# Embedding, projections and out-projection around a first attention as streams of four tiles, with constant rows kept on chip

## The reference

```python
h = _L0_tok_ref(x, emb, Wq, bq, Wk, bk, Wv, bv, Wo, bo)
#   e = emb[x]; q, k, v = e @ W.T + b, 16 heads of 16
#   softmax(0.25 * q @ k.T) @ v, then @ Wo.T + bo
h = h + _L0_attn_ref(_layernorm(h), Wq, ..., Wqs, bqs, Wks, bks, Wvs, bvs, temp)
#   the same with a score of 16 + 3 products for each head:
#   three more come from small projections of q, k and v
#   (k-part and v-part crossed)
```

## Time and profile before

| | us |
|---|---|
| median of 3 runs | 4443.97 (4440.75 to 4445.12) |
| the profiled execution | 4443.18, span 4441.2 |
| start to the first score matmul | 128.0 |
| first attention | 408.4 |
| between the attentions | 198.6 |
| second attention | 408.6 |
| the rest | 3297.6 |

### The profile page before, as it was taken

One profiled execution on the slowest core, in us unless ns is written; L12 is line 12 of the kernel. 1 busy time (PEld: TensorE's weight loads), 2 busy tenths in 40 slices (PEclk: granted clock), 3 DMA queues, 4 the chain that ended last, 5 costly groups with the idle time before them and its releaser, 6 DMA issues. The chain is left out here.

```text
span 4441.2 us, 98171 instructions
## 1 busy us (share of the span) xinstructions
PE 4048.9 (91%) x33142; PEld 2813.6 (63%) x33144; DVE 3197.5 (72%) x5533; ACT 2627.5 (59%) x7011; POOL 1930.9 (43%) x1276
## 2 busy tenths in 40 slices
PE   4899967999445699999999999999999999999997
PEld 2566633666313377777777777777777777777776
DVE  3788644888677677777777777777777777777775
ACT  1476522677231476666666666666666666666664
POOL 2000010000000566666566666665666666666663
PEclk9899987999777899999999999999999999999999
DMA  4222023221010310021011110111001100111001
GB/s 114 73 54 57 21 66 81 55 53 48 20 40 29 104 23 18 20 59 40 18 23 46 46 27 18 39 41 40 20 21 49 51 18 20 51 42 29 20 18 48
DMA packets 101814, 184.23 MB, mean 41 GB/s; under 512 B 25173, under 2 KB 59121, under 8 KB 100977
## 3 DMA queue, kind: packets, MB, share of 16 engines
q1 hardware_dynamic: 100592, 176.37, 14.9%
q0 software_dynamic: 768, 2.10, 0.3%
HBM read 99.51 MB, written 25.17 MB: 28 GB/s over the span
## 5 line engine op out<-in xcount | busy, mean ns | idle before, releaser
L1542 POOL TENSOR_TENSOR swp<-raw,table 128x512 f32<-128x512 f32 x384 | 481.1, 1275 | 635.0 <-DVE ss L1953 634.9
L705 DVE TENSOR_REDUCE maxima<-PS 128x1 f32<-128x512 f32 x1024 | 631.6, 680 | 129.9 <-PE PS L539 129.5
L1625 PE MATMUL PS<-wqk,xT 128*128 128x512 f32 x1536 | 686.5, 600 | 5.7 <-DMA wqk<-in_L_ffn_Wqkv 4.4
L1572 POOL TENSOR_TENSOR probs<-probs,prob_recip 128x512 f32<-128x512 f32 x384 | 472.7, 1250 | 437.5 <-DVE prob_recip L2011 437.5
L1882 ACT ACTIVATE probs<-probs,neg 128x128 f32<-128x128 f32 x1536 | 595.9, 389 | 27.1 <-DVE neg L2005 25.6
L669 ACT ACTIVATE probs<-PS 128x512 f32<-128x512 f32 x1024 | 519.2, 602 | 153.8 <-PE PS L553 153.3
L1552 POOL TENSOR_TENSOR rinv<-ssm,power 128x32 f32<-128x32 f32 x96 | 526.9, 5489 | 0.0
L1625 PEld LDWEIGHTS PS<-wqk,xT 128*128 128x128 f32 x1536 | 283.7, 190 | 336.0 <-issue 253.0
L1728 PE MATMUL PS<-xnT,w 128*128 128x128 f32 x3840 | 476.9, 275 | 0.4 <-DVE hidden L2071 0.4
L539 PE MATMUL PS<-k_stack,q_stack 128*128 128x512 f32 x1024 | 428.1, 438 | 36.4 <-DMA k_stack<-L_attn_qk 17.8
L1728 PEld LDWEIGHTS PS<-xnT,w 128*128 128x128 f32 x3840 | 452.3, 192 | 1.4 <-issue 0.7
(11 more groups left out here) (231 smaller groups left out, 8089.2 us busy)
## 6 DMA issues: line engine op xcount, KB each, us to landing
V_window<-V SPq DMA_DIRECT2D x180, 256.0 KB, 2.8
wqk<-in_L_ffn_Wqkv SPq DMA_DIRECT2D x12, 1024.0 KB, 6.4
w<-in_L_ffn_W SPq DMA_DIRECT2D x18, 640.0 KB, 4.7
q_stack<-L_tok_qk SPq DMA_DIRECT2D x128, 80.0 KB
k_stack<-L_tok_qk SPq DMA_DIRECT2D x128, 80.0 KB
q_stack<-L_attn_qk SPq DMA_DIRECT2D x128, 80.0 KB
k_stack<-L_attn_qk SPq DMA_DIRECT2D x128, 80.0 KB
wv<-in_L_ffn_Wqkv SPq DMA_DIRECT2D x6, 1024.0 KB, 5.1
```

The lines of the kernel that those rows point to most:

```text
L705: dve.tensor_reduce(maxima[:, k // 2, k % 2:k % 2 + 1], SM(r, k), AX.X, ALU.max).then_inc(sm_maxed, 1)
L1542: pool.tensor_tensor(swp[:, w, :, a:a + LD // 2], raw[:, w, :, b:b + LD // 2], table[:, j % 2, 2 + w, a:a + LD // 2].rearrange("p (o d) -> ...
L1572: pool.tensor_tensor(view, view, psr[:, 4 * q:4 * q + 4].rearrange("p (h o) -> p h o", o=1) .to_broadcast([P, 4, P]), ALU.mult).then_inc(p ...
L1625: mm = pe.matmul(wide(kind, half, j), xT[:, k, at:at + P], rhs, start=(k == 0), stop=(k == DC - 1))
```

## The change

The two attentions now share one scope (`attentions`) with one `V`, `q_stack` and `k_stack`.

- `token_projections` is one block in place of six: ids are loaded first, then the identity and all weights, also those of the second attention; gathers have a semaphore for each pair of tiles; transposes, copies, projections and values follow chunk by chunk. Clears move off GpSimd: ACT writes zeros to both stacks, DVE clears `V`.
- The constant rows are no longer stored to HBM and loaded. DVE writes ones into partitions 96 to 127 of `k_stack` once; the low block's loads overwrite the first of them. The row of the maxima goes to partition 127 of `q_stack`, and the matmul for the maxima leaves that partition out (`KMAX`). The scratch tensors have 16 rows a head in the first attention, 19 in the second, and each load copies that many.
- The loads of the first six heads (48 DMAs) are issued at the end of the projection block; `attend` skips them.
- `spin_projections` is one block for out-projection of the first attention, layernorm, transposes, projections and extra products of the second, chunk by chunk.
- `output_projection` at the end adds the bias to `H` ahead of its wait for PE.

Core of the diff:

```diff
-ROWS = 20
+def stack_loads(c, eng, at, scratch, it, r, rows, loaded):
+    qs, ks = at
+    for blk in range(4):
+        for dst, part in ((qs, blk // 2), (ks, 2 + blk % 2)):
+            eng.dma_start(dst[32 * blk:32 * blk + rows, r, :].bitcast(F32),
+                          scratch[part, bass.ds(it, 1), 0:rows, :].rearrange("o r s -> (o r) s")).then_inc(loaded[r], 16)
...
+def token_projections(c, V, qs, ks, scratch, loaded, w, spin_w):
...
+                    sp.dma_start(ids[:, :], ins["x"].rearrange("b (t p) -> p (b t)", p=P)).then_inc(ids_loaded, 16)
+                    sp.dma_start(c.ident[:, :], ins["identity"]).then_inc(ident_loaded, 16)
...
+                    load_output_weights(c, sp, "L0_tok", w, wo_loaded)
+                    load_spin_weights(c, sp, spin_w)
+                for n, (ch, which, m) in enumerate(units):
+                    b, off = ch // 2, (ch % 2) * CH
+                    it0 = b * HEADS + m * HPC
+                    for half, (src, ready) in enumerate(((high, qk_high), (low, qk_low))):
+                        sp.wait_ge(ready, n + 1)
+                        sp.dma_start(scratch[2 * which + half, it0:it0 + HPC, 0:HD, off:off + CH],
+                                     src[:, n % 2, :].bitcast(F32)).then_inc(stored[n % 2], 16)
+                for u in range(2):
+                    sp.wait_ge(stored[u], 32 * len(units) // 4)
+                sp.wait_ge(cleared, 3)
+                for r in range(RING):
+                    stack_loads(c, sp, (qs, ks), scratch, r, r, HD, loaded)
...
+                turn(0)
+                turn(1)
+                for ch in range(CHUNKS):
+                    for u in range(4):
+                        query_key(4 * ch + u)
+                        if u in (0, 2) and ch + 1 < CHUNKS:
+                            turn(2 * ch + 2 + u // 2)
+                        if u in (1, 3):
+                            values(2 * ch + u // 2)
...
+                act.activation(qs[:, :, :].rearrange("p r (a f) -> p (r a) f", f=P), nothing, ACT.Copy, scale=0.0).then_inc(cleared, 1)
+                act.activation(ks[:, :, :].rearrange("p r (a f) -> p (r a) f", f=P), nothing, ACT.Copy, scale=0.0).then_inc(cleared, 1)
...
+                    act.wait_ge(qk_done, n + 1)
+                    wait(act, qk_low, n - 1)
+                    wait(act, stored[n % 2], 32 * (n // 2))
...
+                    if ch == 0:
+                        dve.wait_ge(cleared, 2)
+                        dve.memset(ks[96:P, :, :].bitcast(F32), 1.0).then_inc(cleared, 1)
...
+def spin_projections(c, V, qs, ks, scratch, loaded, context, w, s):
...
+                    if n % 4 == 3:
+                        for which2 in range(2):
+                            sp.wait_ge(spin_split, 2 * ch + which2 + 1)
+                            for half, src in enumerate((s_high, s_low)):
+                                for comp in range(3):
+                                    sp.dma_start(scratch[2 * which2 + half, b * HEADS:(b + 1) * HEADS, HD + comp, off:off + CH],
+                                                 src[32 * comp:32 * comp + HEADS, which2, :].bitcast(F32)).then_inc(spin_stored, 16)
...
+                for r in range(RING):
+                    stack_loads(c, sp, (qs, ks), scratch, r, r, HD + 3, loaded)
...
+                out_chunk(0)
+                out_chunk(1)
+                turn("x", 0)
+                turn("x", 1)
+                pe.wait_ge(s["loaded"], 16 * SPIN_LOADS)
+                out_chunk(2)
+                project_chunk(0)
+                turn("x", 2)
+                turn("x", 3)
+                out_chunk(3)
+                project_chunk(1)
...
+def attentions(c):
...
+        first = nc.dram_tensor("tok_qk", (4, ITERS, HD, SEQ), F32, kind="Internal").ap()
+        second = nc.dram_tensor("spin_qk", (4, ITERS, HD + 3, SEQ), F32, kind="Internal").ap()
...
-                wait(sp, st_done, UNITS * (it - RING) + UNITS)
-                for blk in range(4):
-                    for dst, part in ((qs, blk // 2), (ks, 2 + blk % 2)):
-                        sp.dma_start(dst[32 * blk:32 * blk + ROWS, r, :].bitcast(F32),
-                                     scratch[part, bass.ds(it, 1), :, :].rearrange("o r s -> (o r) s")).then_inc(loaded[r], 16)
+                sp.wait_ge(st_done, UNITS * (it - RING) + UNITS)
+                stack_loads(c, sp, (qs, ks), scratch, it, r, rows, loaded)
...
-                sp.dma_start(qs[0:1, r, :].rearrange("o (a t) -> o a t", a=QT).bitcast(F32),
+                sp.dma_start(qs[P - 1:P, r, :].rearrange("o (a t) -> o a t", a=QT).bitcast(F32),
...
-                if h0:
+                if h0 and not (isinstance(t, int) and t < RING):
                     load(h0)
...
-                pe.matmul(SM(r, k), qs[:, r, q * P:(q + 1) * P], ks[:, r, half * CH:(half + 1) * CH],
+                pe.matmul(SM(r, k), qs[0:KMAX, r, q * P:(q + 1) * P], ks[0:KMAX, r, half * CH:(half + 1) * CH],
```

More of the change, by code:

```diff
@@ L60, in wait @@
     eng.wait_ge(sem, value)
[L63 to L112, removed]
 def layernorm(c, src, dst, eps=EPS):
@@ L196, in softmax_attention @@
[L196 to L227, removed]
@@ new lines, in attentions @@
+        s["stacks"], s["sbias"], s["factor"] = c.sb(outer, "spin_w", [P, 5, DC, 96]), c.sb(outer, "spin_b", [96, 5]), c.sb(outer, "factor", [P, 1])
+        s["loaded"] = c.sem("spin_loaded")
+        first = nc.dram_tensor("tok_qk", (4, ITERS, HD, SEQ), F32, kind="Internal").ap()
+        second = nc.dram_tensor("spin_qk", (4, ITERS, HD + 3, SEQ), F32, kind="Internal").ap()
+        with nc.cleanup_on_exit():
+            loaded = [c.sem(f"stack_loaded{r}") for r in range(RING)]
+            token_projections(c, V, qs, ks, first, loaded, w, s)
+            attend(c, V, qs, ks, first, loaded, context, HD)
@@ new lines, in attentions, with output_projection, tile_of, _ @@
+        with nc.cleanup_on_exit():
+            loaded = [c.sem(f"stack_loaded{r}") for r in range(RING)]
+            spin_projections(c, V, qs, ks, second, loaded, context, w, s)
+            attend(c, V, qs, ks, second, loaded, context, HD + 3)
+            output_projection(c, context, w["next"])
+def output_projection(c, context, w):
+    nc = c.nc
+    with ExitStack() as ctx:
+        CT = c.sb(ctx, "CT", [P, DC, TOK])
+        def tile_of(t, k):
+            b, q = t // QT, t % QT
+            return context[:, q, b * D + k * P:b * D + (k + 1) * P]
+        to_feature_major(c, tile_of, CT)
+        projected, added, biased = c.sem("projected"), c.sem("added"), c.sem("biased")
+        with nc.Block() as block:
+            @block.tensor
+            def _(pe):
+                for t in range(TILES):
+                    wait(pe, added, t - 3)
+                    for k in range(DC):
+                        mm = pe.matmul(c.PS[:, t % 4, 0:D], CT[:, k, t * P:(t + 1) * P], w["wo"][:, k, :],
+                                       start=(k == 0), stop=(k == DC - 1))
+                    mm.then_inc(projected, 1)
+            @block.vector
+            def _(dve):
+                for t in range(TILES):
+                    dve.tensor_tensor(c.H[:, t, :], c.H[:, t, :], w["bo"][:, :], ALU.add).then_inc(biased, 1)
+                    dve.wait_ge(projected, t + 1)
+                    dve.wait_ge(biased, t + 1)
+                    dve.tensor_tensor(c.H[:, t, :], c.PS[:, t % 4, 0:D], c.H[:, t, :], ALU.add).then_inc(added, 1)
@@ L431, in attend @@
+def attend(c, V, qs, ks, scratch, loaded, context, rows):
     nc = c.nc
```

632 lines of the change are left out of this document (439 added, 193 removed).

## The result

The kernel after takes 4779.56 us (median of 4 runs, 4777.89 to 4782.04) against 4442.36 us (4 runs, 4438.96 to 4445.12) of the kernel before on the same chip: a ratio of 1.076, with a 95% interval of 1.0741 to 1.0779. The forecast was 4,789.5. The profiled execution of after took 4778.97 us, its span is 4777.2.

The account below looks back on a forecast made before the run. TensorE was taken to fill both attentions, the stages around them not. First score 101.5, attention 408.4, loads from 636.9, 32 heads x 25.4 us and 39.5 end at 1,489.5, +345.5: 4,789.5 us; range 4,704 to 5,000.

Parts of the forecast that it names:

- the height of the load: Second attention: 19-row loads, 19 being prime, use one DMA engine where 20 rows used ten; loads set the pace.
- The price of 25.4 us a head: Second attention: one engine at 24.5 GB/s takes 25.4 us for a head's loads, over the 12.00 us step.
- SP stays ahead, no gap: Second attention: SP issues load t+1 while head t is still landing, so the one engine never idles.
- The start: Before the first attention: first score at 101.5 instead of 128.03 us, gain 26.5, bounds 15 and 38.
- give nothing by themselves: Removed constant-row DMAs, 16 at the first attention and 4 at the second: beside the stall, no gain of their own.
- the stall: Before each attention's projections: DVE held 13.91 us in a 128x2 multiply by GpSimd's clears; moving these ends it.
- Between the attentions: Stage before the second attention: last spin stores issued near 127 us after it began, bounds 115 and 150.
- the end of the last head: Second attention: 39.5 us from the last head's first score to the attention's end.
- (a): Second attention: 19-row copies spread over ten or more engines after all, a gain of 78 us, 4,366; chance 0.08.
- (b): Second attention: single engine keeps only 15.3 GB/s, 41 us a head, 5,288; chance 0.10 for 28 to 41 us.
- (c): Second attention: maxima's row queues behind one more load, a step becomes 25.4 + 12.0 us, 5,173; chance 0.04.
- (d): Start: 48 issues (19.7 us) eat the early block's gain, which falls from 26.5 to 15; no chance given.

Follow-up runs that it names:

- the two runs on the kernel before: Kernel before with GpSimd's clears held until DVE's small multiply has run: 4421.37 us; the same with constant rows sent one behind each unit's stores: 4425.63 us.

## Why the prediction was right, and where it was not

**The step that decided, the height of the load, held in sign, mechanism and size.** One engine, share 0.06 to 0.07, steps of 23 to 28 us released by a DMA. TensorE was forecast busy under 60%; it is 55% from the first load on (462 us of 642 to 1,478), 65% from the first score matmul on. The price of 25.4 us a head was mis-sized by 1.7 us: 23.7 measured, 26.3 GB/s, close to the row of 26.8 GB/s with long rows and above the middle that was taken. Over 32 heads that is 53 us too much.

**"SP stays ahead, no gap" was wrong.** It is the step that failed. It held in the loop, but not at the block's end: SP is stopped in the issue while six or so loads are out, the block holds back the first score matmul until the last of 48 has been taken, and then the engine is dry for about 30 us (786 to 816). Including smaller pauses behind it the loads took 795.2 us, from 642.04 to 1,437.24, where 32 x 23.74 is 759.7; so 35.5 us of gap that had not been forecast. It covers two thirds of the error in the price. The forecast was 9.9 us off the median, less than either of these errors: that it came so near is luck, because the two have opposite signs. Without the gap the same forecast would have been some 45 us too high.

**The start** was forecast at 101.5 and came at 99.26. Its parts were less exact than its sum:

```profile
5.98 3.26 DVE L294 MEMSET V<- 128x3840 f32 x1 [0.72 <-issue]
6.71 3.42 POOL L195 DMA_INDIRECT X<-in_L_tok_emb,row  x1 [0.30 <-issue]
...
23.76 0.69 ACT L258 ACTIVATE whole<-PS,bqs 128x512 f32<-128x512 f32 x1 [8.79 <-issue]
...
75.52 0.33 SPq L180 DMA_DIRECT2D tok_qk<-low  x1
...
98.27 0.42 SPq L132 DMA_DIRECT2D k_stack<-tok_qk  x1
```

The first eviction is at 23.76, not near 20: the second gather takes 3.42 us in place of about 1, and chunk 0 waits for the fourth (its second pair of transposes runs at 17.91). Then the first four products of 512 columns take 3.75 us (from 19.90), where the next four take 2.06 (from 24.30). The last store is issued at 75.52, not 80.8: the sixteen units go at about 3.3 us (23.76 to 73.43 for fifteen of them), for the 3.51 of the earlier trace rows. And the 48 issues end at 98.7, 22.7 us for the 19.7 forecast, 0.46 us each while sixteen engines take part.

**The constant rows "give nothing by themselves"** was only half right, and the two runs on the kernel before show why: with the stall in place they were covered, with the stall gone 6.7 us of the 12.8 gained at the first eviction are lost again by the first score. Since the change takes both away, the sum did not suffer.

**Between the attentions** the loads begin 134 us after the end of the first attention (507.98 to 642.04), not 127. The first eviction is 28 us into the stage, not 22:

```profile
522.91 3.65 PE L438 MATMUL PS<-wo,CT 128*128 128x256 f32 x8 [3.30 <-DVE H L601]
...
535.74 0.78 ACT L553 ACTIVATE whole<-PS,bqs,factor 128x512 f32<-128x512 f32 x1 [6.21 <-PE PS L447]
```

The third chunk of the out-projection waits 3.30 us for its PSUM bank, because DVE, which has to free it, is first at the layernorm of chunk 0. The forecast named this bank and gave it no such wait; it is about half of the 6 us. The rounds after it took 29.7, 24.4 and 24.6 us, near the 29 and 25 to 26 of the forecast (535.74, 565.45, 589.80, 614.39).

**The sum**, by its own terms: start -2.2, first attention +0.3, this stage +7.1, the rate -53.1, the pause +35.5, the end of the last head +1.3 (40.8 for 39.5), the rest of the program +2.0 (1.6 more than before where 0.4 less was forecast). That is -9.1; the profiled execution was 9.7 under the forecast for it, and the difference is rounding of the forecast's figures and the 0.2 us by which the time outside the span differs.

**The rivals.** (a), all loads spread, was given 4,366; the version with twenty rows and all else as in after took 4371.4. It is the change's worth without the fault. (b) and (c), a slower engine and a queueing maxima row, did not show. (d), the issues that eat the start's gain, was right that the issues take from the start's gain, but not in its number: with twenty rows the first score comes at 81.42 with one head ahead and at 97.89 with six, yet the gain at the start was 28.8 us and not 15.

## What to carry to other kernels

Before a transfer is made smaller, look at the two outermost sizes it will have: here a row less per load (20 to 19) turned ten DMA engines into one and cost 408 us, and a row more, zeros, was the whole cure. Where a block's end waits for the engine that issues loads, put in it only the loads that the next stage needs at once: each further head cost 1.6 to 3.7 us an attention here while issues were quick. Where they were not, each held the block 23.7 us longer, and the three heads more cost 32.8 us there in all, since their loads had to be done in any case. And removing a wait shows the price of what had stood beside it; a part that "costs nothing" has to be priced again once its cover is gone.

## What the runs showed of the hardware

- **An issuing engine can be held inside an issue.** With single-engine loads of 19 rows of 4 KB, SP took 0.25 to 0.50 us for each of the first six and then 5.54 us for every second one, the time in which two landed. With twenty rows (ten engines) the issues took 0.3 to 0.4 us each. That it is a full queue that holds SP is a reading of these times and not shown; how many loads it takes was not measured apart.
- **One DMA engine moves 26 to 27 GB/s** with 4 KB rows from HBM (17 and 19 rows alike), though nine together gave 130 GB/s, ten 154, 15.3 each, and sixteen 139, 8.7 each. What bounds the ten wasn't tried, nor whether the sixteen were held by SP's issues (64 KB every 0.46 us is 142 GB/s) or held them.
- **The stores got quicker with the layout.** In the 16-row scratch tensor a store's issue takes 0.33 us, and in a stretch with stores alone more than eight engines are at work. The second attention's stores in the same kernel are alike but for the 19 rows a head of their tensor: 0.60 us, and eight engines, as in the kernel before. With 20 rows a head the issue takes 0.60 us too. So the rows a head that the tensor has make the difference; that they have to be as many as are stored is a guess from 16, 19 and 20.

```profile
66.00:72.00 6.00, 6.00 (x20) 3.41 (x19) 2.65 (x5) 2.81 (x5) 0.00 (x0) 1.00 0.69 262
598.00:604.00 6.00, 6.00 (x19) 3.04 (x18) 2.52 (x5) 3.64 (x7) 0.00 (x0) 1.00 0.49 154
```

- **A gather issued by GpSimd took 3.42 us beside a DVE memset.** The memset of `V` runs from 5.98 to 9.24 us; the gather that began at 6.71 ends at 10.13, 0.89 us after the memset, and the other gathers of this kernel and of the one before take 0.94 to 1.30 us. The same pair of durations, 3.26 and 3.41 to 3.43, came back in the versions above that share this code. That the memset holds the gather isn't shown, because no run parts them. The Trainium skill (SBUF — State Buffer, "SBUF: two separate sides") has the locking of the two engines for DVE's two-port instructions, and for a DVE instruction outside those modes with at most one SBUF input it has none; this trace doesn't tell which of the two the memset is.
